# Position groups of the stationary query rows taken at every eighth position, and both halves of a step shifted by GpSimd

## What is computed

```python
q, k, v = (shape_heads(x @ W + b) for W, b in ((Wq, bq), (Wk, bk), (Wv, bv)))   # 16 heads of 8
scores = einsum('bhsd,bhkd->bhsk', q, k) / sqrt(8 * 3)
c2p = einsum('bhsd,hkd->bhsk', q, pos_k)            # content to position
scores += take_along_axis(c2p, clip(rel + 32, 0, 63)) / sqrt(8 * 2)
p2c = einsum('bhsd,hkd->bhsk', k, pos_q)            # position to content
scores += take_along_axis(p2c, clip(-rel + 32, 0, 63)).swapaxes(-1, -2) / sqrt(8 * 2)
probs = softmax(scores)
ctx = einsum('bhsk,bhkd->bhsd', probs, v)           # then @ Wo + bo
```

## Time and profile before

| | us |
|---|---|
| median of 3 runs | 1697.88 |
| lowest, highest | 1676.09, 1705.04 |
| the profiled execution: time | 1695.65 |
| its span, first to last instruction | 1693.7 |
| busy: PE, DVE, ACT, POOL | 1054.5, 886.0, 674.0, 491.3 |
| mean share of 16 DMA engines, SP's queue | 52.6% |

### The profile page before, as it was taken

How to read it: one execution, slowest core, us unless ns; L and a number is a source line. 1 busy time by engine, 2 the same in 40 slices (tenths; PEclk the granted TensorE clock), 3 DMA queues, 4 the chain that set the end, 5 groups by cost and what they waited for, 6 DMA issues and landing times. The chain is left out here.

```text
span 1693.7 us, 32133 instructions
## 1 busy us (share of the span) xinstructions
PE 1054.5 (62%) x8740; PEld 774.0 (46%) x8740; DVE 886.0 (52%) x2997; ACT 674.0 (40%) x1563; POOL 491.3 (29%) x504
## 2 busy tenths in 40 slices
PE   4965178662357656665765666666576576672676
PEld 3854067541234434444443444444344344362676
DVE  6877545563344544454454445445445454654455
ACT  2354034353234434443543444444344444321333
POOL 4212356310222222232222223223222222301564
PEclk9985589876578877887878788788788888765899
DMA  6800433317776666766676676666667667303331
GB/s 161 164 1 2 177 93 105 92 47 251 103 91 101 118 92 97 101 113 95 103 110 98 93 101 117 94 101 117 96 102 112 99 102 106 45 1 131 102 105 50
DMA packets 113730, 168.93 MB, mean 100 GB/s; under 512 B 16361, under 2 KB 68656, under 8 KB 113168
## 3 DMA queue, kind: packets, MB, share of 16 engines
q1 hardware_dynamic: 108048, 155.65, 52.6%
q0 software_dynamic: 5632, 12.70, 2.2%
HBM read 66.68 MB, written 35.55 MB: 60 GB/s over the span
## 5 line engine op out<-in xcount | busy, mean ns | idle before, releaser
L1261 POOL TENSOR_SCALAR ds_p2c<-ds_p2c,ds_max 128x256 f32<-128x256 f32 x256 | 271.3, 1060 | 748.7 <-DVE ds_max L1505 748.6
L1410 ACT ACTIVATE ds_stage<-ds_bank 128x512 f32<-128x512 f32 x256 | 139.0, 594 | 383.5 <-DMA ds_c2p<-ds_stage 243.6
L1498 DVE TENSOR_TENSOR ds_p2c<-ds_c2p,ds_p2c 128x512 f32<-128x512 f32 x256 | 184.3, 720 | 181.2 <-DMA ds_c2p<-ds_stage 181.2
L1505 DVE CUSTOM_DVE_ANT_0 ds_p2c<-ds_bank,ds_p2c 128x256 f32<-128x256 f32 x512 | 195.9, 419 | 102.0 <-PE ds_bank L1335 101.2
L1291 PE MATMUL ds_bank<-ds_tab,d_qkr 64*64 64x256 f32 x2048 | 169.2, 450 | 72.0 <-DMA d_qkr<-scratch_qk 50.6
L1446 ACT ACTIVATE all_xt<-ds_bank 128x512 f32<-128x512 f32 x256 | 153.5, 600 | 76.2 <-PE ds_bank L1346 74.3
L1346 PE MATMUL ds_bank<-all_constants,ds_p2c 128*128 128x128 f32 x1024 | 181.3, 307 | 3.9 <-ACT all_xt L1446 1.9
L1364 PE MATMUL ds_bank<-all_constants,ds_values_t 128*128 128x128 f32 x128 | 35.7, 371 | 223.4 <-ACT ds_values_t L1441 223.4
L1291 PEld LDWEIGHTS ds_bank<-ds_tab,d_qkr 64*64 64x64 f32 x2048 | 101.0, 198 | 120.8 <-issue 91.3
L1335 PE MATMUL ds_bank<-ds_ks,ds_qs 72*128 72x256 bf16 x512 | 114.9, 312 | 57.1 <-DVE ds_max L1505 57.1
L1346 PEld LDWEIGHTS ds_bank<-all_constants,ds_p2c 128*128 128x128 f32 x1024 | 142.9, 162 | 13.5 <-DVE ds_p2c L1512 3.5
(11 more groups left out here) (274 smaller groups left out, 1855.1 us busy)
## 6 DMA issues: line engine op xcount, KB each, us to landing
ds_c2p<-ds_stage SPq DMA_DIRECT2D x256, 128.0 KB
ds_c2p<-ds_stage SPq DMA_DIRECT2D x128, 256.0 KB
ds_tab<-scratch_tables SPq DMA_DIRECT2D x64, 248.0 KB, 6.0
slots_in<-all_zero SPq DMA_DIRECT2D x2, 5180.0 KB, 39.0
ds_qs<-scratch_q_parts SPq DMA_DIRECT2D x32, 288.0 KB
ds_ks<-scratch_k_parts SPq DMA_DIRECT2D x96, 96.0 KB
d_qkr<-scratch_qk SPq DMA_DIRECT2D x512, 8.0 KB
0fe_xb<-slots_in SPq DMA_DIRECT2D x40, 129.5 KB, 2.1
```

Source lines behind the costliest of these rows:

```text
L1261: pool.tensor_scalar(PC[half][:, 1, b, :], PC[half][:, 1, b, :], mx[:, 2 * b + 1:2 * b + 2], None, ALU.subtract).then_inc(s_sub1, 1)
L1410: act.activation(STAGE[:, 2 * (where % 2) + swap, :], pc[swap][:, :], ACT.Copy).then_inc(s_cc, 1)
L1498: dve.tensor_tensor(z, CT[half][:, b, :, :], z, ALU.add).then_inc(s_z, 1)
L1505: last = dve.tensor_tensor_reduce(out=PC[half][:, st, b, :], in0=pqk[b % 2][:, st * SEQ:(st + 1) * SEQ], in1=PC[half][:, st, b, :], scale= ...
```

## The change

Two things are changed, both in the third layer.

**Position groups.** A group of 16 query positions is no longer 16 neighbours but every eighth position of a tile of 128: positions n, n+8, ..., n+120. The projected queries are written to that order (`by_position` and `by_batch`, keys as before), the query table of partition block s is shifted by 8s instead of s elements (its rows are 391 elements long instead of 496: `TABLE_Q`), the window's start `c` on TensorE changes with it, and the transfers from `STAGE` to `CT` now have as destination every eighth partition: 8 partitions over a span of 57 for L1217, 16 over a span of 121 for L1221. Number, size and order of the matrix products, copies and transfers stay.

**The shift.** GpSimd subtracts the maximum from both parts of a step, one instruction for each, and VectorE's `shift` is gone.

```diff
+TABLE_Q = OFFS - 1 - 8 * 15
 ...
             if j == 0:
-                return QT[j][:, :].rearrange("p (h s b n) -> p h s n b", h=2, s=16, n=NB16)[:, half, :, :, b:b + 2]
+                return QT[j][:, :].rearrange("p (h s u n) -> p h s u n", h=2, s=16, n=NB16 // 2)[:, half, :, 2 * b:2 * b + 4, :]
 ...
-        def by_batch(part):
+        def by_batch(j, part):
+            if j == 0:
+                return part.rearrange("p (u s n) -> p s u n", u=4, s=16)
             return part.rearrange("p (b n s) -> p s n b", b=2, s=16)
 ...
-        "tables": [bass.AP(tensor=tab, offset=j * P * OFFS, ap=[[1, 16], [OFFS, P], [1, TABLE]]) for j in range(2)],
+        "tables": [bass.AP(tensor=tab, offset=j * P * OFFS, ap=[[(8, 1)[j], 16], [OFFS, P], [1, (TABLE_Q, TABLE)[j]]]) for j in range(2)],
 ...
-                    at = 16 * (2 * i) + 8 * (1 - r)
-                    sp.dma_start(CT[half][at:at + 8, :, :, :]..., STAGE[64 * r:64 * (r + 1), 2 * (i % 2), :])
+                    at = 2 * i + 64 * (1 - r)
+                    sp.dma_start(CT[half][at:at + 57:8, :, :, :]..., STAGE[64 * r:64 * (r + 1), 2 * (i % 2), :])
 ...
-                at = 16 * (2 * i + 1)
-                sp.dma_start(CT[half][at:at + 16, :, :, :]..., STAGE[:, 2 * (i % 2) + 1, :])
+                at = 2 * i + 1
+                sp.dma_start(CT[half][at:at + 121:8, :, :, :]..., STAGE[:, 2 * (i % 2) + 1, :])
 ...
-                        pool.tensor_scalar(PC[half][:, 1, b, :], PC[half][:, 1, b, :], mx[:, 2 * b + 1:2 * b + 2], None, ALU.subtract).then_inc(s_sub1, 1)
+                        for st, s_sub in enumerate((s_sub0, s_sub1)):
+                            pool.tensor_scalar(PC[half][:, st, b, :], PC[half][:, st, b, :], mx[:, 2 * b + st:2 * b + st + 1], None, ALU.subtract).then_inc(s_sub, 1)
 ...
-                            c = TABLE - SEQ - 16 * g
+                            c = SEQ - 1 - 8 * 15 - P * st - (2 * where + swap)
 ...
-                if before:
-                    shift(*before)
 ...
-            shift(HB - 1, 1, HALF - 1)
```

More of the change, by code:

```diff
@@ L932, in _ @@
                                    bias=b_col[:, j:j + 1], scale=float(scale[j])).then_inc(s_p1, 1)
-                    act.activation(by_position(j, g), by_batch(bank[n % 4][:, :]), ACT.Identity,
+                    act.activation(by_position(j, g), by_batch(j, bank[n % 4][:, :]), ACT.Identity,
                                    bias=b_col[:, j:j + 1], scale=float(scale[j])).then_inc(s_qe, 1)
@@ L1192, in load_tables @@
                 for j in range(2):
-                    sp.dma_start(TAB[half][:, j, :], views["tables"][j][:, bass.ds(head * DB, DB), :]).then_inc(s_tab[half], 16)
+                    sp.dma_start(TAB[half][:, j, 0:(TABLE_Q, TABLE)[j]], views["tables"][j][:, bass.ds(head * DB, DB), :]).then_inc(s_tab[half], 16)
             def load_rows(head, half, first, count):
@@ L1215, in spread @@
                 for r in range(2):
-                    at = 16 * (2 * i) + 8 * (1 - r)
-                    sp.dma_start(CT[half][at:at + 8, :, :, :].rearrange("p b t k -> p (b t k)"), STAGE[64 * r:64 * (r + 1), 2 * (i % 2), :]).then_inc(s_ct[i % 2], 16)
+                    at = 2 * i + 64 * (1 - r)
+                    sp.dma_start(CT[half][at:at + 57:8, :, :, :].rearrange("p b t k -> p (b t k)"), STAGE[64 * r:64 * (r + 1), 2 * (i % 2), :]).then_inc(s_ct[i % 2], 16)
                 sp.wait_ge(s_cc, CC * u + 2 * i + 2)
                 sp.sem_inc(s_go_sp, 1)
-                at = 16 * (2 * i + 1)
-                sp.dma_start(CT[half][at:at + 16, :, :, :].rearrange("p b t k -> p (b t k)"), STAGE[:, 2 * (i % 2) + 1, :]).then_inc(s_ct[i % 2], 16)
+                at = 2 * i + 1
+                sp.dma_start(CT[half][at:at + 121:8, :, :, :].rearrange("p b t k -> p (b t k)"), STAGE[:, 2 * (i % 2) + 1, :]).then_inc(s_ct[i % 2], 16)
             def heads(head, last):
@@ L1260, in heads @@
                         pool.sem_inc(s_go_pool, 1)
-                        pool.tensor_scalar(PC[half][:, 1, b, :], PC[half][:, 1, b, :], mx[:, 2 * b + 1:2 * b + 2], None,
-                                           ALU.subtract).then_inc(s_sub1, 1)
+                        for st, s_sub in enumerate((s_sub0, s_sub1)):
+                            pool.tensor_scalar(PC[half][:, st, b, :], PC[half][:, st, b, :], mx[:, 2 * b + st:2 * b + st + 1], None,
+                                               ALU.subtract).then_inc(s_sub, 1)
             pool.wait_ge(s_bo, 16)
@@ L1494, in results, with scores @@
                                   rec[:, :, :].unsqueeze(3).to_broadcast([P, 2, 4, DB]), ALU.mult).then_inc(s_ctx, 1)
-            def scores(step, half, b, before):
+            def scores(step, half, b):
                 z = PC[half][:, :, b, :]
                 dve.tensor_tensor(z, CT[half][:, b, :, :], z, ALU.add).then_inc(s_z, 1)
-                if before:
-                    shift(*before)
                 dve.wait_ge(s_z, step + 3)
@@ L1508, in scores @@
                 last.then_inc(s_sc, 1)
-            def shift(head, half, b):
-                dve.wait_ge(s_sc, number(head, half, b) + 3)
-                dve.tensor_scalar(PC[half][:, 0, b, :], PC[half][:, 0, b, :], mx[:, 2 * b:2 * b + 1], None, ALU.subtract).then_inc(s_sub0, 1)
             def heads(head, last):
@@ L1522, in heads @@
                     for b in range(HALF):
-                        scores(HALF * u + b, half, b, steps_before(head, half, b, 1))
+                        scores(HALF * u + b, half, b)
                         if b % 4 == 0 and (before := group_before(head, half, b, 8)):
```

## The result

The changed kernel takes 1502.67 us (median of four runs, 1500.81 to 1506.33) against 1693.1 us for the kernel before in the same session (1676.09 to 1705.04). The ratio is 0.8908 with an interval of 0.8833 to 0.8982. The forecast was 1555 us with a range of 1460 to 1640 and a chance of 0.83 for faster: sign, mechanism and range held, but the gain is 190 us and not 142. The profiled execution took 1506.33 us around a span of 1504.4, which answers to the earlier trace rows with 189.3 us less.

What follows compares the result with a forecast made beforehand. The prediction took a loop to bound each half: SP's start, C0's transfers, C2's copy, scores, SP's next start. 1695.65 - 127 (halves) - 7 (first half) - 8 (shift) = 1553.7, about 1555 us; range 1460 to 1640.

Steps and rivals of the forecast that it cites:

- A: Stretch of a half from SP's first issue to ScalarE's C2 copy: forecast to fall from 18.3 to 14.2 us.
- The rate of an engine: Transfers from `STAGE` to `CT`: a busy DMA engine was to go from 7.9 to 16.8 GB/s with spread destinations.
- The price of C0's transfers: From C0's first issue to C2's copy, 9.97 us before: 3.3 us less for each piece.
- B at 14.25: Stretch of a half from C2's copy to SP's next start: forecast to stay at 14.25 us.
- ScalarE's readiness: Ahead of C2's copy: ScalarE ready 11.95 us after SP's start, leaving 2.2 us to cover GpSimd's 1.19 us delay.
- The first half: -7: VectorE's first `z` waits 11.51 us for four pieces in two rounds: 2 x 3.3, so -7 us.
- The shift: -8: VectorE's shift in a half's last step: 0.35 us saved, 0.1 given back, 32 x 0.25 = -8 us.
- Edits at nothing: Shorter query table rows, TensorE windows at any element and copies before `attend`: taken as 0, copies bounded by 3 us.
- The transfers gain nothing: Rival: engines slow for another reason, such as reading `STAGE`; 1688 us, up to 1726 without cover; chance 0.12.
- spread destinations are dearer: Rival: writes to far partitions lose the run over neighbours, slowing engines; 1880 us at half rate; chance 0.05.
- The loop opens: Rival: ScalarE no longer waits for pieces, needing C0's 9.97 us to fall under 4.4; 1452 us, chance 0.12.
- GpSimd holds VectorE up: Rival: each `z` of B stands through a whole GpSimd instruction, up to 89 us; 1644 us, chance 0.07.

Runs made afterwards that it cites:

- The experiment on the destinations: Kernel before with only the destination partitions of the `STAGE` to `CT` transfers changed to every eighth, rows landing at wrong positions: 1517.18 us, ratio 0.8956.
- C0 first: Changed kernel with C0's three transfers issued before the table loads and first four row loads of each half: 1408.14 us, ratio 0.8297.
- Shift alone: Kernel before with both shifts on GpSimd, groups and transfers as before: 1694.08 us, ratio 1.0021.

## Why the prediction came out as it did

**What bounds the kernel: right.** The loop through C0's transfers and C2's copy was the limit. The experiment on the destinations moved A alone, and C0 first moved it again by the amount that the loop gives.

**The rate of an engine: right.** 16.8 GB/s was taken from the tables; 16.2 were measured. An engine's 48 KB thus take 3.0 us instead of 6.2.

**The price of C0's transfers: too small a gain.** The step "3.3 us less for each piece" made 9.97 into 6.67; measured are 5.60 and 5.69. The engines' own work accounts for 6.2 - 3.0 = 3.2. The other 1.1 is what still lay in the engines' queues when C0 was issued. In the kernel before, just ahead of C0's own packets (722.4 to 724 us):

```profile
DMA packets 165, 0.26 MB, mean 161 GB/s; under 512 B 22, under 2 KB 165, under 8 KB 165
q1 hardware_dynamic: 165, 0.26, 60.1%
```

and in the changed kernel in the same place (692.6 to 694 us):

```profile
DMA packets 37, 0.03 MB, mean 19 GB/s; under 512 B 11, under 2 KB 28, under 8 KB 37
q1 hardware_dynamic: 37, 0.03, 7.8%
```

Before, the engines were busy at 60% with loads that had piled up behind the slow pieces of the half before; now they stand ready. I had counted this backlog only for the long halves. With SP's way shorter by 0.2 it makes 13.0 us for A on average instead of 14.2, and 31 x 1.2 = 37 us of the 48 that the prediction fell short by. The tables, issued just ahead of C0, show the same queue (KB each, median us from issue to landing), in the kernel before and in the one whose destinations alone lie eight apart:

```profile
ds_tab<-scratch_tables SPq DMA_DIRECT2D x64, 248.0 KB, 6.0
```

```profile
ds_tab<-scratch_tables SPq DMA_DIRECT2D x64, 248.0 KB, 3.9
```

There the tables are the old ones, so their shorter rows in the changed kernel aren't the reason. That the backlog makes up the 1.1 is a reading of these rows; no run took it away by itself.

**B at 14.25: right**, 14.34 in the row and 27.25 - 12.98 = 14.3. TensorE's clock falls after ScalarE's wait as before, to a mean of 0.76 in B where it was 0.67; the same product in TensorE's timeline, to be held against the earlier trace rows:

```profile
701.29 2.08 PE L1333 MATMUL ds_bank<-d_qkr,ds_tab 64*128 64x128 f32 x16 [1.07 <-DVE ds_p2c L1488]
...
707.57 1.16 PE L1333 MATMUL ds_bank<-d_qkr,ds_tab 64*128 64x128 f32 x16
```

ScalarE's wait of 4.12 to 4.53 us is left, and with it the fall of the clock, so nothing came of the 29 us that a steady clock was to bring. C0 first got part of them: B is 12.6 us there in halves at a clock of 1.00.

**ScalarE's readiness: 3.3 us too late.** The prediction has ScalarE ready 11.95 us after SP's start, so that a wait of 2.2 is left in an A of 14.2. A became shorter than that and the wait still longer. ScalarE's last work ahead of the C2 copy at 698.14:

```profile
693.45 0.58 ACT L1452 ACTIVATE all_xt<-ds_bank 128x512 f32<-128x512 f32 x1
```

It ends at 694.03, 8.68 us after SP's start at 685.35. This half's first `z` waits 1.20 us instead of 5.35, and ScalarE's two waits for TensorE ahead of C2 in the kernel before (1.92 us at 723.19 and 1.32 at 725.10) are gone. The prediction left VectorE's wait out of its sum, which was right, but it didn't see that ScalarE would be ready the earlier for it. So the cover for GpSimd's delay was about 4 us and not 2.2.

**The first half: -7 was -12.2.** From the first issue of `CT` to the first `z` it is 17.82 us instead of 29.98. The first `z`'s own wait, in VectorE's timeline, is 5.57 where the earlier trace rows has 11.51:

```profile
437.22 0.69 DVE L1504 TENSOR_TENSOR ds_p2c<-ds_c2p,ds_p2c 128x512 f32<-128x512 f32 x1 [5.57 <-DMA ds_c2p<-ds_stage]
```

**The shift: -8 was nothing that shows.** Shift alone gave 1.0021, and VectorE's shift put back 0.8919 where the changed kernel has 0.8908. Two rows show where the 0.35 us went. They are from the lists of groups (count; busy us, mean ns; idle before), to be held against the earlier trace rows:

```profile
L1267 POOL TENSOR_SCALAR ds_p2c<-ds_p2c,ds_max 128x256 f32<-128x256 f32 x512 | 483.5, 957 | 364.6 <-DVE ds_max L1509 364.6
L1504 DVE TENSOR_TENSOR ds_p2c<-ds_c2p,ds_p2c 128x512 f32<-128x512 f32 x256 | 202.5, 791 | 42.2 <-ACT ds_p2c L1428 25.9
```

`z` takes 0.79 us instead of 0.72, and the sum behind it waits 0.22 to 0.27 us for its own `z`; so 0.35 us saved in the last step are nearly all given back (0.07 and 0.22 to 0.27). I had given back 0.1.

**GpSimd doesn't bound: right.** It idles 364.6 us before its shifts, and TensorE's transposes wait 3.9 us for it over the whole run. It holds VectorE up only a little. VectorE's and GpSimd's timelines around one half's start:

```profile
688.64 0.80 DVE L1504 TENSOR_TENSOR ds_p2c<-ds_c2p,ds_p2c 128x512 f32<-128x512 f32 x1
...
690.36 0.69 DVE L1504 TENSOR_TENSOR ds_p2c<-ds_c2p,ds_p2c 128x512 f32<-128x512 f32 x1
```

```profile
688.43 1.82 POOL L1267 TENSOR_SCALAR ds_p2c<-ds_p2c,ds_max 128x256 f32<-128x256 f32 x2 [1.34 <-DVE ds_max L1509]
```

The `z` at 688.64 began inside the first of two GpSimd instructions of about 0.9 us and took 0.80, the one at 690.36 began ahead of the next one and took 0.69. Of the 124 `z` that begin inside an instruction of GpSimd with 0.7 us or more of it left, 122 end within 0.1 us behind it and take 0.80 to 0.92, so these overlaps cost 0.1 to 0.2 us. One other fares worse. It meets GpSimd's addition of two operands in SBUF (first two lines, the changed kernel), and so does one in the kernel before (last line):

```profile
445.32 5.42 DVE L1504 TENSOR_TENSOR ds_p2c<-ds_c2p,ds_p2c 128x512 f32<-128x512 f32 x1
```

```profile
442.04 8.14 POOL L1271 TENSOR_TENSOR all_rows<-all_rows,d_bo 128x4096 f32<-128x4096 f32 x1 [76.53 <-DMA d_bo<-in_L_attn_b_bo]
```

```profile
456.13 5.55 DVE L1498 TENSOR_TENSOR ds_p2c<-ds_c2p,ds_p2c 128x512 f32<-128x512 f32 x1
```

The `z` at 445.32 ends at 450.74, 0.56 us after GpSimd's instruction (450.18). By the rule of the Trainium skill (SBUF — State Buffer, Who interferes with whom) a `z` that comes second stands until the other is done. The long instruction bears this out: 5.42 us instead of 0.69. The short ones do so only in part, since a `z` that stood for all of the rest and then took its 0.69 us would have needed 1.4 at 688.64 and not 0.80. The prediction looked at a short one alone. Its rival had no price here because the long instruction stands in the kernel before as well, and the shifts are short.

**Edits at nothing: right.** ScalarE's copies into the new order became shorter (16.4 us for the 16 with that shape before, 12.4 after). The stretch up to the first issue of `CT` is 2.5 us longer all the same (416.87 to 419.40), and 5.2 us went after the last score. Neither can be put down to the edits: over the traces of all experiments the first stretch ends between 416.1 and 423.6 us, and the last takes 208.2 to 216.2 with the same code. TensorE's products with windows at any element take 464 ns instead of 450, but 463 where only the destinations differ and the windows are the old ones, so the windows cost nothing that shows.

**The account.** Up to the first issue +2.5, to the first `z` -12.2, from there to the last score -174.5, behind it -5.2: -189.3 us, rounded at the end. The large term is 30 halves at -5.4, 162.5 together, and -12.0 from the first `z` to the next head's first waiting C2; that the first head gained more than the others wasn't explained.

**The rivals.** "The transfers gain nothing" and "spread destinations are dearer" are refuted by the destinations alone. "The loop opens" did not come with this change. Its condition of 4.4 us was too mild: with ScalarE ready at 694.03 and C0 issued at 692.54, C0 to C2's copy would have to fall to 1.5 us, and it took 5.6. It came with C0 first, which moves the issue and not the transfers. "GpSimd holds VectorE up" has no measurable price, by shift alone.

## What to carry to other kernels

Where transfers within SBUF are slow, look at the destination partitions before the bytes: a share near half the engines with each at half its usual rate was the sign, and steps of four between the partitions cost nothing here. When a transfer in a loop gets faster, count what was queued ahead of it too, since that queue shrinks as well. And a transfer that an engine waits for belongs ahead of loads that nobody is waiting for; here that was worth another 94.5 us.

## What the runs showed of the hardware

- 8 and 16 neighbouring destination partitions about halve a DMA engine's rate for packets of 2 KB: 7.9 against 16.2 GB/s in two short windows, 8.9 against 15.9 (230 and 129 ns a packet) from 500 to 1150 us. Packets and bytes are the same, and 8.6 against 10.5 engines are busy in the windows.
- Two apart does as well as eight apart (5.77 and 5.69 us from issue to copy), four apart better (5.03); a packet of 2 KB takes 132, 129 and 111 ns.
- Spreading the transfer of 256 KB alone, two apart, brings 59% of what spreading all three two apart brings.
- An addition of two SBUF operands on VectorE that begins inside a GpSimd shift of 0.9 us takes 0.80 to 0.92 us instead of 0.69. One that began inside GpSimd's own addition of two SBUF operands (8.14 us) took 5.42.
- With a granted clock of 1.00, 0.87 and 0.76 in it, stretch B takes about 12.6, 13.2 and 14.0 to 14.4 us in the halves of the kernel with C0 first.
